# Layer 2's first token group mixed inside the last two tiles of layer 1, the last products of layer 1 inside the first units of layer 2, and the class rows read one unit sooner

## The reference, cut to what matters

```
x = x + ffn0(cond0(x))   # a convolution; a low-rank mixture (base_W, LoRA, top 2 of 28 experts)
x = x + ffn1(cond1(x))   # out = einsum('boi,bih->boh', agg_w, x) + agg_b; int8 fake-quantised linear
x = x + ffn2(cond2(x))   # the same mixing; gate, up = x@Wg.T, x@Wu.T; (silu(gate)*up)@Wd.T, M = 1792
x = x + ffn3(cond3(x))   # the same mixing; a router over 3 experts (top 2 by the first token of a row)
# mixing: agg_w, agg_b come from an MLP of the condition, one 32x32 matrix and one bias per batch row
```

## Time and profile before

| what | us |
|---|---|
| median of 3 runs (760.94 to 766.59) | 761.42 |
| the profiled execution | 761.69 |
| its span, first to last instruction | 760.0 |
| TensorE busy in it | 742.8 |
| VectorE, GpSimd, ScalarE busy | 454.8, 349.8, 301.4 |
| mean granted clock of TensorE | 0.99 |

### The profile page before, as it was taken

How to read it: one execution, slowest core, us unless ns; L and a number is a source line. 1 busy time by engine, 2 the same in 40 slices (tenths; PEclk the granted TensorE clock), 3 DMA queues, 4 the chain that set the end, 5 groups by cost and what they waited for, 6 DMA issues and landing times.

```text
span 760.0 us, 11094 instructions
## 1 busy us (share of the span) xinstructions
PE 742.8 (98%) x3588; PEld 598.4 (79%) x3604; DVE 454.8 (60%) x1047; ACT 301.4 (40%) x578; POOL 349.8 (46%) x381
## 2 busy tenths in 40 slices
PE   8999999999899999999999999998999999999997
PEld 5588887776688888888888888877788887888886
DVE  2566776668623244773567445886578788555443
ACT  6444444443532334243434334231454354434331
POOL 2756667766435613120221015868454645554540
PEclk9799999999999999999999999999999999999999
DMA  9447455634132102210211102423512212221200
GB/s 282 78 84 186 163 168 169 185 119 153 43 138 85 54 0 86 110 28 1 84 61 51 29 24 73 168 57 110 182 43 98 84 43 61 67 79 48 70 28 28
DMA packets 45255, 68.82 MB, mean 91 GB/s; under 512 B 21784, under 2 KB 22040, under 8 KB 44936
## 3 DMA queue, kind: packets, MB, share of 16 engines
q1 hardware_dynamic: 35440, 37.87, 17.0%
q0 software_dynamic: 9152, 29.69, 12.7%
q10 hardware_dynamic: 608, 0.55, 0.2%
HBM read 44.94 MB, written 17.66 MB: 82 GB/s over the span
## 4 chain that ended last, share of the span: by engine, by line
PE 86%; DVE 10%; ACT 2%; issue 2%; DVEq 0%; ACTq 0%
PE bank L2101 24%; PE bank L1957 11%; PE bank L2052 11%; PE bank L2084 11%; PE bank L1771 8%; PE bank L1705 4%; PE bank L1809 3%; PE bank L2063 2%; PE bank L1841 1%; DVE junk L1410 1%; PE bank L1977 1%; PE bank L1821 1%; PE bank L1917 1%; PE bank L1722 1%; PE bank L1716 1%
## 5 line engine op out<-in xcount | busy, mean ns | idle before, releaser
L1562 DVE TENSOR_TENSOR sil<-bank,sil 128x512 f32<-128x512 f32 x56 | 38.6, 690 | 98.0 <-PE bank L2101 98.0
L2101 PE MATMUL bank<-th,wgr 128*128 128x512 f32 x224 | 88.8, 396 | 1.9 <-POOL tl L570 1.8
L2101 PE MATMUL bank<-th,wur 128*128 128x512 f32 x224 | 88.0, 393 | 0.0
L2101 PE MATMUL bank<-tl,wgr 128*128 128x512 f32 x224 | 87.8, 392 | 0.0
L2101 PE MATMUL bank<-tl,wur 128*128 128x512 f32 x224 | 87.7, 391 | 0.0
L1957 PE MATMUL bank<-wda,hh 128*128 128x512 f32 x224 | 87.5, 391 | 0.0
L1957 PE MATMUL bank<-wda,hl 128*128 128x512 f32 x224 | 87.2, 389 | 0.0
L2052 PE MATMUL bank<-wda,xch 128*128 (+1 forms) x272 | 84.5, 392 | 1.8 <-DVE xcl L1588 1.8
L1075 ACT ACTIVATE hh<-sil 128x512 fp32r<-128x512 f32 x56 | 35.4, 632 | 116.7 <-DVE sil L1562 116.7
L1067 ACT ACTIVATE sil<-bank 128x512 f32<-128x512 f32 x56 | 33.4, 597 | 96.7 <-PE bank L2101 96.6
L1564 DVE TENSOR_TENSOR hl<-sil,hh 128x512 fp32r<-128x512 f32 x56 | 45.2, 808 | 39.1 <-ACT hh L1075 39.1
(11 more groups left out here) (347 smaller groups left out, 1806.0 us busy)
## 6 DMA issues: line engine op xcount, KB each, us to landing
tap<-in_x_taps_dram SPq DMA_DIRECT2D x16, 260.0 KB, 2.9
xin<-in_x_rows_dram SPq DMA_DIRECT2D x16, 256.0 KB, 2.9
xd<-xo SPq DMA_DIRECT2D x16, 256.0 KB, 3.2
xc<-xd SPq DMA_DIRECT2D x16, 256.0 KB, 3.9
xres<-xd SPq DMA_DIRECT2D x4, 1024.0 KB, 5.5
xd<-xres SPq DMA_DIRECT2D x4, 1024.0 KB, 5.2
tsd<-tf SPq DMA_DIRECT2D x4, 1024.0 KB, 4.4
raw<-in_w_dram POOLq DMA_DIRECT2D x16, 256.0 KB, 3.0
```

The costliest lines, as they stand in the source:

```text
L1562: v.tensor_tensor(hf[:, m % 2], p_pre[(2 * m + 1) % 3][:], sil[:, m % 2], ALU.mult).then_inc(s_hf, 1)
L2101: last = mm(p_pre[(2 * m + b) % 3][:], w[:, (m * KT + kt) * P:(m * KT + kt + 1) * P], x[:, kt], start=(kt == 0 and n == 0), stop=(kt == KT ...
```

## The change

1. Group 0 of layer 2 is mixed as the other groups are, by `cond2(0, j)` into bank 0: tiles 0 and 1 in the step of tile 14 (before and after `lora(14)`), tile 2 after `router(15)`, tile 3 after `base(15)`. `cond` is gone, and so are `bias23` with its DMA, `t_rows`, `t_hi` and GpSimd's `t_lo`. ScalarE writes the four mixed tiles with `rows2_out`, two into the upper half of `xres`, two into `tf` (`rows2`). `features_t(0)` transposes blocks 0, 1, 3 after `hidden(15)` and block 2 after `lora(15)`.
2. The `xc` tiles 2 and 3 of group 0 are rounded by ScalarE (`x_hi`) between the `rows2_out` of tiles 0 and 1, and their low parts (`x_lo`) stand on VectorE at the end of the step of tile 14. SyncE's loads of them stand in the same place of its queue as before, behind `store_x2(12)`.
3. `integers_t(14)` and `mix1(15)` go between gate 0 and up 0 of layer 2, `linear1(14)` behind up 0. On VectorE `t_lo_p(0)` (now all four blocks of `tl`) stands ahead of `row_sum_0(15)`, and `scaled_back(14)` and `quantised(15)` behind unit 0.
4. The blocks are used in the order 0, 1, 3, 2 (`KT_ORDER`) in all groups.
5. `classes(c)` stands behind `route_two(c)` at m = 8, and in the last group `ranks(0)` and `order_one(0)` at m = 9, one unit sooner; `permutation(0)` stays at m = 11.

TensorE issues 48 matmuls of 128 columns less, and 12 of 512 columns and 16 transposes more.

```diff
+        def rows2(c, j):
+            return tf[:, j] if c or j >= 2 else xres[:, j + 2]
@@ -406,11 +407,11 @@
                         sp.wait_ge(d_st1[p], 16 * GT // 2)
                     load_xc(0, 0)
                     load_xc(0, 1)
-                    load_bias()
-            sp.wait_ge(s_xch, 2)
-            sp.wait_ge(s_xclp, 2)
-            load_xc(0, 2)
-            load_xc(0, 3)
+                if n == TILES - 1:
+                    sp.wait_ge(s_xch, 2)
+                    sp.wait_ge(s_xclp, 2)
+                    load_xc(0, 2)
+                    load_xc(0, 3)
             store_x2(TILES - 3)
             store_x2(TILES - 2)
@@ -954,27 +950,22 @@
                 act.wait_ge(s_gf, n + 1)
                 nc.scalar.activation(bdh[:], bdf[:], ACT.Copy).then_inc(s_gh, 1)
-            def t_hi():
-                for kt in range(KT):
-                    act.wait_ge(s_tf, kt + 1)
-                    nc.scalar.activation(th[:, kt], tf[:, kt], ACT.Copy).then_inc(s_th, 1)
             def t_hi_p(c):
-                for kt in range(KT):
-                    act.wait_ge(s_tr2, (c - 1) * KT + kt + 1)
+                for n, kt in enumerate(KT_ORDER):
+                    act.wait_ge(s_tr2, c * KT + n + 1)
                     nc.scalar.activation(th[:, kt], p_pre[kt][:], ACT.Copy).then_inc(s_th, 1)
             def rows2_out(c, j):
                 act.wait_ge(s_cond, c * GT + j + 1)
-                if j == 0 and c == 1:
-                    act.wait_ge(s_tlp, 2)
-                    act.wait_ge(s_tld, 2)
+                if j == 0 and c == 0:
                     act.wait_ge(d_tab, 16 * 6 * BPT)
+                elif j == 0 and c == 1:
+                    act.wait_ge(s_tr2, KT)
                 elif j == 0:
                     act.wait_ge(d_tsd, 16 * (c - 1))
                     act.wait_ge(s_lg, (c - 1) * GT)
-                nc.scalar.activation(tf[:, j], bank[3][:], ACT.Identity,
+                nc.scalar.activation(rows2(c, j), bank[3 if c else 0][:], ACT.Identity,
                                      bias=bcol23[:, c * GT + j:c * GT + j + 1]).then_inc(s_te2, 1)
@@ -991,6 +982,9 @@
                 if t == TILES - 2:
                     x_hi(0, 0, 16, False)
                     x_hi(0, 1, 16, False)
+                if t == TILES - 1:
+                    rows2_out(0, 2)
+                    rows2_out(0, 3)
                 if t == 0:
                     mixed(1)
@@ -1004,18 +998,18 @@
                     mixed1(t - 1)
                 if t == 9:
                     diag_hi(0)
+                if t == TILES - 2:
+                    for j in range(2):
+                        rows2_out(0, j)
+                        x_hi(0, j + 2, 32)
                 if t == 0:
                     mixed(2)
             for t in range(TILES):
                 step(t)
-            x_hi(0, 2, 32)
-            x_hi(0, 3, 32)
-            integers_t(TILES - 2)
+            t_hi_p(0)
             x1_hi(TILES - 1)
             diag_hi1(TILES - 1)
-            t_hi()
-            mixed1(TILES - 1)
             def x3_hi(c, j):
@@ -1065,14 +1059,18 @@
                     if m >= 2:
                         act.wait_ge(s_hl, s * MT + m - 1)
                     nc.scalar.activation(sil[:, m % 2], p_pre[2 * m % 3][:], ACT.Silu).then_inc(s_sil, 1)
-                    if s == 0 and m == 1:
-                        integers_t(TILES - 1)
+                    if s == 0 and m == 0:
+                        integers_t(TILES - 2)
                     if s >= 1 and m == 8:
                         route_exp(c)
                     act.wait_ge(s_hf, s * MT + m + 1)
                     if m >= HSLOTS:
                         act.wait_ge(s_down, s * MT + m - HSLOTS + 1)
                     nc.scalar.activation(hh[:, m % HSLOTS], hf[:, m % 2], ACT.Copy).then_inc(s_hh, 1)
+                    if s == 0 and m == 0:
+                        mixed1(TILES - 1)
+                    if s == 0 and m == 1:
+                        integers_t(TILES - 1)
                     if s >= 1 and m == 0:
                         diag_hi(2 * s)
@@ -1332,6 +1334,8 @@
                         v.tensor_copy(wq[:, k], bank[6 - k // 2][:].bitcast(BF16)[:, (k % 2) * D:(k % 2 + 1) * D]).then_inc(s_wqc, 1)
                 if t >= 2:
                     scaled_back(t - 2)
+                if t == TILES - 2:
+                    x_lo(0)
             weight_scales()
-            def t_rows():
-                dve.wait_ge(s_cond, GT)
-                dve.wait_ge(d_bias, 16)
-                def lo(kt):
-                    dve.wait_ge(s_th, kt + 1)
-                    v.tensor_tensor(tl[:, kt], tf[:, kt], th[:, kt].bitcast(F32), ALU.subtract).then_inc(s_tld, 1)
-                for kt in range(KT):
-                    v.tensor_tensor(tf[:, kt], p_pre[kt][:], bias23[:], ALU.add).then_inc(s_tf, 1)
-                    if kt == 2:
-                        lo(1)
-                lo(3)
             def t_lo_p(c):
-                for kt in range(KT):
-                    dve.wait_ge(s_th, c * KT + kt + 1)
+                for n, kt in enumerate(KT_ORDER):
+                    dve.wait_ge(s_th, c * KT + n + 1)
                     v.tensor_tensor(tl[:, kt], p_pre[kt][:], th[:, kt].bitcast(F32), ALU.subtract).then_inc(s_tld, 1)
@@ -1380,12 +1364,8 @@
             quantised(TILES - 2)
-            x_lo(0, (2,))
+            t_lo_p(0)
             row_sum_0(TILES - 1)
-            x_lo(0, (3,))
-            t_rows()
-            scaled_back(TILES - 2)
-            quantised(TILES - 1)
             route = Chain(dve, ch_rt)
@@ -1562,6 +1542,9 @@
                     v.tensor_tensor(hf[:, m % 2], p_pre[(2 * m + 1) % 3][:], sil[:, m % 2], ALU.mult).then_inc(s_hf, 1)
                     dve.wait_ge(s_hh, s * MT + m + 1)
                     v.tensor_tensor(hl[:, m % HSLOTS], hf[:, m % 2], hh[:, m % HSLOTS].bitcast(F32), ALU.subtract).then_inc(s_hl, 1)
+                    if s == 0 and m == 0:
+                        scaled_back(TILES - 2)
+                        quantised(TILES - 1)
                     if s >= 1 and 3 <= m < 7:
                         logits(c, m - 3)
@@ -1569,9 +1552,8 @@
                         others(c)
                     if s >= 1 and m == 8:
                         route_two(c)
-                    if s >= 1 and m == 9:
                         classes(c)
-                    if s == LAST and m == 10:
+                    if s == LAST and m == 9:
                         order_one(0)
                     if s == LAST and m == 11:
@@ -1877,75 +1859,63 @@
                     mix1(t - 1)
                 if t >= 2:
                     linear1(t - 2)
+                if t == TILES - 2:
+                    cond2(0, 0)
                 lora(t)
-            for t in range(TILES - 1):
-                step(t)
-            def cond(tiles, last_tile=False):
-                pe.wait_ge(s_gl, 1)
-                for j in tiles:
-                    if j < 2:
-                        pe.wait_ge(s_xclp, j + 1)
-                    else:
-                        pe.wait_ge(s_xcld, j - 1)
-                    for kt in (0, 1, 3, 2):
-                        if j == 0 and kt == 2 and last_tile:
-                            pe.wait_ge(s_htl, TILES)
-                        cols = slice(kt * P, (kt + 1) * P)
-                        xp = (xch[:, j % 2, cols], xcl[:, j % 2, cols])
-                        for n, (x, w) in enumerate(parts(xp, (bdh[:, j], bdl[:, j]))):
-                            last = mm(p_pre[kt][:, j * P:(j + 1) * P], x, w, start=(n == 0), stop=(n == 2))
-                    last.then_inc(s_cond, 1)
+                if t == TILES - 2:
+                    cond2(0, 1)
             def cond2(c, j):
-                pe.wait_ge(s_gl, 2 * c)
+                pe.wait_ge(s_gl, max(2 * c, 1))
                 if j < 2:
                     pe.wait_ge(s_xclp, c * 2 + j + 1)
                 else:
                     pe.wait_ge(s_xcld, c * 2 + j - 1)
                 if j:
-                    pe.wait_ge(s_te2, (c - 1) * GT + j)
+                    pe.wait_ge(s_te2, c * GT + j)
+                elif c == 0:
+                    pe.wait_ge(s_cvs, TILES)
                 elif c == 1:
-                    pe.wait_ge(s_tf, KT)
+                    pe.wait_ge(s_tld, KT)
                 else:
                     pe.wait_ge(s_clsd, c - 1)
                 for k, (w, y) in enumerate(parts((bdh[:, j], bdl[:, j]), (xch[:, j % 2], xcl[:, j % 2]))):
-                    last = mm(bank[3][:], w, y, start=(k == 0), stop=(k == 2))
+                    last = mm(bank[3 if c else 0][:], w, y, start=(k == 0), stop=(k == 2))
                 last.then_inc(s_cond, 1)
-            def features_t(c):
-                pe.wait_ge(s_te2, c * GT)
-                for kt in range(KT):
+            def features_t(c, kts=KT_ORDER):
+                pe.wait_ge(s_te2, (c + 1) * GT)
+                for kt in kts:
+                    if c == 0 and kt == 2:
```

(35 more changed lines are left out.)

33 lines of the change are left out of this document (13 added, 20 removed).

## The result

| | median us | runs |
|---|---|---|
| before | 763.55 | 11 |
| after | 770.84 (767.41 to 772.57) | 11 |
| ratio | 1.0087, 95% 1.0066 to 1.0109 | |
| profiled execution of after | 770.2, span 768.5 | clock 0.986 |

The change makes the kernel slower by 0.9%. The prediction compares with a median of 761.42 from three runs of the kernel before, which now has 763.55 from eleven, so it is held against this result as a ratio.

What follows compares the result with a forecast made beforehand. TensorE, busy for 98% of the span, was taken to bound the kernel. Layer 1's end 5.2, clock 1.0 and class rows 0.1 gave +6.3 us on 761.69, 768.0; less 0.27 to the median, 767.7, range 762.8 to 770.6.

Steps and rivals of the forecast that it cites:

- The work on TensorE: Matmuls removed (5.4 us) against matmuls (2.7) and transposes (1.8) added: -0.9 us.
- the loads: Tile 14's step: ScalarE, then VectorE, wait for a load behind tile 12's store; hidden(15) starts 6.8 us later.
- rival B: Layer 1's end: loads hold nothing, row sum 3.3 us late instead of 6.5; +2.0, 763.4 to 764.5 us; chance 0.15.
- From hidden(15) to the first down product: Layer 1's end into layer 2: 22.4 us with gaps of 5.1, where before took 24.0; -1.6 us.
- Both parts: The stretch up to layer 2's first down product, loads' +6.8 and the -1.6 after hidden(15) together: +5.2 us.
- The clock: Granted clock falls behind the new gaps of 3.0 and 2.65 us; second fall taken in full, +1.0 us.
- The class rows: Layer 2's last group: ranks(0) waits 2.2 us for cls, permutation(0)'s 1.92 goes, the clock's fall moves to unit 10; +0.1 us.
- rival C: As forecast, but the clock never falls, nor in layer 2's last group: +3.6, 765.0 us; chance 0.17.
- From there on layer 2's next instructions stand to each other as before: Behind layer 2's first down product the order of its next instructions is unchanged; no cost was given.

Runs made afterwards that it cites:

- e7: e6 with VectorE's classes(c) put ahead of route_two(c) as well; 757.5 us, ratio 0.993 to the kernel before.
- e3: The changed kernel with the loads of mixed tiles 2 and 3 ahead of tile 12's store in SyncE's queue; 765.29 us, ratio 1.005 to the kernel before.
- e5: The changed kernel with VectorE's row sum of tile 15 ahead of the four low parts of group 0; 769.02 us, ratio 1.0071 to the kernel before.
- a0: The changed kernel measured again, nothing altered; 769.98 us against 762.38 for the kernel before, ratio 1.0087.
- e8: The changed kernel with layer 3's fourth gather held until the last group's residual adds are done; 767.42 us, ratio 1.0046 to the kernel before.
- e2: The changed kernel with the class rows put back where they were, so the mixing alone; 765.13 us, ratio 1.005 to the kernel before.
- e4: The changed kernel with VectorE's classes(c) ahead of route_two(c) in every group; 764.2 us, ratio 1.0053 to the kernel before.
- e1: The kernel before with only the class rows moved sooner; 761.76 us against 761.28, ratio 1.0004.
- e6: The changed kernel with e3's loads and with VectorE's, TensorE's and ScalarE's orders at layer 1's end mended; 762.78 us, ratio 0.9986 to the kernel before.
- e9: e6 with layer 3's fourth gather held until the last group's residual adds are done; 761.66 us, ratio 0.9971 to the kernel before.
- e11: e7 with layer 3's first two gathers one split sooner and the fourth gather held; 759.31 us, ratio 0.9924 to the kernel before.
- e10: e7 with layer 3's first two gathers issued one split sooner; 757.88 us, ratio 0.9916 to the kernel before.

## Why the prediction was right, and where not

The measured ratio, 1.0087, lies by 0.05% of the time from the predicted 767.7 / 761.42 = 1.0082, inside the range (762.8 to 770.6, or 1.0018 to 1.0121). The absolute time, 770.84, lies 0.2 above that range, since the kernel before, too, measured 2.1 above the base of 761.42. The steps held unequally, and that the ratio came out so near is luck in part.

**The work on TensorE, -0.9, and the loads, +6.8: right.** The two blocks removed took 2.91 + 2.93 us of TensorE's time (from 187.95 and from 192.59 in before); in e7, whose clock is full there, the four mixed tiles and the transposes take 3.1 + 1.8, so -0.9. Load issued at 182.83 (said 182.5, and this whole run is 0.3 late from its start), row sum at 187.94 (187.9), gap 2.64 (3.0), `hidden(15)` at 194.91 (194.6). e3 moved the loads alone and took 3.3 us out of exactly this stretch; rival B had priced that at 3.2. The rounding starts 2.75 us after the load's issue, where I took 2.9 from the rows.

**From hidden(15) to the first down product, -1.6: right** (22.32 against 24.01, -1.7), with the gaps at 1.26 (said 1.4), 2.23 (2.65) and 0.40 (0.65). e5 showed the cause of the second: with the row sum ahead of the low parts it is gone. Both parts came to +5.15 where 5.2 was said.

**The clock, +1.0: wrong in the profiled run.** The first fall came and was largely hidden in the wait for the third mixed tile, as said (a0, without it, is 0.2 us shorter from `hidden(14)` to `hidden(15)`). The second, the term itself, did not: after and a0 have the clock at 1.00 behind the 2.23 us gap, e3 and e8 have it at half behind the same gap, 1.3 and 1.8 us of it reaching the first down product. Over the six profiles with this gap (e2 and e4 have no fall either) that is 0.5 us in the mean and not 1.0.

**The class rows, +0.1: right as a mean** (e1: +0.3 at full clock, 1.0004). In the profiled run the fall expected in unit 10 failed to come and the result is -1.6, where the other end named was -1.7. So up to layer 3's first transposes the run is rival C: they stand 3.86 us later than before (538.04 and 534.18), 0.3 of it from the start, where C said 3.6.

**The step that failed** is the one that ended the account there: "From there on layer 2's next instructions stand to each other as before", and behind the class rows nothing but the clock was priced. Layer 3's start costs 4.3 us more than before (19.92 against 15.60) in the first profile of the changed kernel and 4.2 more in the second (19.80). What happens there: a signal of TensorE arrives up to 1.9 us late, a gap of 2.5 us opens instead of one of 0.6, and some six microseconds at half clock follow. TensorE also comes to layer 3 sooner after GpSimd's first gather than before, 5.6 us instead of 7.0, but so it does in e1 (5.7), which has no late signal. The kernel loses 5.15 + 0.3 - 1.6 + 4.3 + 0.3 = 8.5 in the profiled run (the two 0.3 are the span's start and its end), where I had 6.3; I came near the ratio because the two falls of the clock that I took in full, 1.0 and 1.7, and that didn't come in this run, stood in for a term that I didn't have. That is luck.

**How far this is shown.** That the late signal recurs is shown: present in after, a0 and e6 in full, in e5, e8, e9 and e11 in part (0.4 to 1.4 us), absent in before, e1 to e4, e7 and e10. With either half of the change alone it is absent, and the halves' ratios, 1.0004 and 1.005, come short of the whole by 0.33%, about 2.5 us; but each interval is 0.25% wide to a side, and in full-clock time the excess is 4.5 - 0.3 - 3.3 = 0.9 us with a standard error of about 0.6, so this excess by itself isn't certain. That the gather's issue causes it is not shown: e8 and e9 speak half for it and e1 against it. What delays the signal, and why neither half alone brings it, stays open.

## What to carry to other kernels

Follow a moved load to its place in its queue, and then ask which engine sits in order behind it: here two loads one store too late cost 3.3 us. With them moved and three orders beside them mended the loss of 0.9% was gone (e6, 0.9986), and with the class counts' place as well it was a gain of 0.7% over the kernel before (e7; 0.8% in e10), a part of which is the late signal's absence. A wait that is removed must be compared with what it is when the engine that causes it meets it otherwise: 1.92 us in one profile, none in another with the same code at that place. After a shift, recheck every place where two engines at their own pace meet, to the end of the program.

## What the hardware showed that I had not expected

- The clock's fall behind a gap on TensorE is no function of the gap alone. Behind the ranks' 2.2 us it fell in e3, e5 and e9 and not in after, a0, e1, e6 and e8; behind `mix1(15)`'s 2.2 us in e3 and e8, not in after, a0, e2 and e4; behind the 2.5 to 2.7 us ahead of `cond2(0, 2)` in after, e2 and e8, not in a0, e4 and e5. At layer 3's start it fell in e4 behind waits of 0.60 and 1.30 us, which e1 and e2 have too, without a fall. In these runs a fall cost 1.3 to 3.4 us where it wasn't hidden.
- A VectorE instruction on a few columns took 1.20 us beside a GpSimd subtraction and 0.14 alone.
- A signal of TensorE reached VectorE and SyncE together 1.9 us late. ScalarE's next signal from TensorE came on time (`xch` at 548.27, where `tokens_t(1)` ends at 548.2), but by then the late one was through, so whether ScalarE would have been late too isn't shown.
- In four profiles the gathered rows were there only 6.5 to 6.7 us after the issue of a broadcast load of 768 KB, with their own gather issued 3.5 to 7.0 us before. Whether the load holds them is not shown.
